# One DMA for the gate and up weights, and the softmax normalisation recorded ahead of the transposes

## What is computed

```python
# DIM 1024, 16 heads of 64, window 256, HIDDEN 3072
q = x @ q_w.T; kv = x @ kv_w.T; k, v = kv[..., :64], kv[..., 64:]
attn = softmax(einsum('bhnwd,bnud->bhnwu', qb, kb) * 64**-0.5)
out  = einsum('bhnwu,bnud->bhnwd', attn, vb)            # per window
x = layernorm(x + out @ proj_w.T + proj_b)
h = silu(x @ w_gate.T / 127) * (x @ w_up.T / 127)       # int8 weights
x = layernorm(x + h @ w_down.T / 127)
```

## Time and profile before

| | |
|---|---|
| two timed runs | 998.68 and 1094.42 us, median 1046.55 us |
| profiled execution, time | 997.76 us |
| its span on the slowest core (core 3 of eight; 987.5 to 995.9 us) | 995.9 us |
| PE busy | 829.3 us (83%) |
| DVE busy | 322.5 us (32%) |
| ACT busy | 241.7 us (24%) |
| POOL busy | 118.1 us (12%) |
| mean granted TensorE clock of a core | 0.89 to 0.90 |

### The profile page before, as it was taken

How to read it: one execution, slowest core, us unless ns; L and a number is a source line. 1 busy time by engine, 2 the same in 40 slices (tenths; PEclk the granted TensorE clock), 3 DMA queues, 4 the chain that set the end, 5 groups by cost and what they waited for, 6 DMA issues and landing times.

```text
span 995.9 us, 12616 instructions; the slowest of 8 cores (987.5 to 995.9 us)
## 1 busy us (share of the span) xinstructions
PE 829.3 (83%) x4288; PEld 362.3 (36%) x4288; DVE 322.5 (32%) x538; ACT 241.7 (24%) x745; POOL 118.1 (12%) x232
## 2 busy tenths in 40 slices
PE   6767776767989999956888899767798999999996
PEld 6123333222434444412333334323243444443332
DVE  0146767332222212102445546533222221111111
ACT  0054545112121111102333334411212111111111
POOL 2000010000222223200000010000122222310000
PEclk9567777797999999977999999778899999999999
DMA  8950120114434445372211130112443444530121
GB/s 117 271 125 12 22 54 1 64 64 137 134 121 129 137 148 157 119 116 51 51 43 43 43 85 33 43 57 79 129 147 107 141 145 150 157 107 32 64 81 68
DMA packets 46957, 94.15 MB, mean 95 GB/s; under 512 B 5552, under 2 KB 5552, under 8 KB 46896
## 3 DMA queue, kind: packets, MB, share of 16 engines
q0 software_dynamic: 37520, 67.91, 26.7%
q1 hardware_dynamic: 9376, 25.43, 7.8%
HBM read 63.44 MB, written 12.58 MB: 76 GB/s over the span
## 4 chain that ended last, share of the span: by engine, by line
PE 64%; DVE 11%; DMA 11%; issue 8%; ACT 5%; DVEq 0%; SPq 0%; POOL 0%; ACTq 0%; POOLq 0%
PE ps L264 60%; DMA wqsb<-wq 5%; PE ps L381 4%; DMA x<-xtm 4%; DVE pool L366 3%; DMA xbf<-xfm 2%; DVE silu L710 2%; ACT r L718 2%; DVE r L710 1%; ACT silu L718 1%; DVE pool L389 1%; DVE x2s L728 1%; DVE pool L320 1%; DVE xbf L456 1%; DVE hbuf L594 1%
## 5 line engine op out<-in xcount | busy, mean ns | idle before, releaser
L264 PE MATMUL ps<-xbf,wuw 128*128 128x512 bf16 x768 | 186.6, 387 | 14.1 <-DVE hbuf L594 14.1
L264 PE MATMUL ps<-xbf,wgw 128*128 128x512 bf16 x768 | 184.3, 383 | 10.6 <-DVE xbf L456 10.6
L264 PE MATMUL ps<-wdres,hbuf 128*128 128x512 bf16 x768 | 186.7, 389 | 7.6 <-PE ps L264 0.3
L594 DVE SCALAR_TENSOR_TENSOR hbuf<-ps,silu 128x512 bf16<-128x512 f32 x96 | 66.4, 692 | 271.7 <-PE ps L264 267.4
L349 ACT ACTIVATE pool<-ps 128x256 bf16<-128x256 f32 x256 | 98.2, 384 | 134.9 <-PE ps L264 89.5
L589 ACT ACTIVATE silu<-ps 128x512 f32<-128x512 f32 x96 | 56.9, 597 | 279.3 <-PE ps L264 279.3
L264 PEld LDWEIGHTS ps<-xbf,wuw 128*128 128x128 bf16 x768 | 75.6, 99 | 108.5 <-issue 21.1
L264 PEld LDWEIGHTS ps<-xbf,wgw 128*128 128x128 bf16 x768 | 75.4, 99 | 104.9 <-issue 19.2
L264 PEld LDWEIGHTS ps<-wdres,hbuf 128*128 128x128 bf16 x768 | 70.6, 99 | 113.3 <-issue 43.8
L564 POOL DMA_DIRECT2D wgw<-wg x96 | 50.8, 529 | 352.4 <-PE ps L264 352.4
L264 PE MATMUL ps<-xbf,wqsb 128*128 128x512 bf16 x256 | 77.4, 445 | 4.1 <-DVE pool L320 0.9
(11 more groups left out here) (55 smaller groups left out, 350.3 us busy)
## 6 DMA issues: line engine op xcount, KB each, us to landing
wgw<-wg POOLq DMA_DIRECT2D x96, 256.0 KB, 2.6
wuw<-wu POOLq DMA_DIRECT2D x96, 256.0 KB, 2.6
x<-xtm SPq DMA_DIRECT2D x16, 512.0 KB, 3.7
y<-x SPq DMA_DIRECT2D x16, 512.0 KB, 2.9
wdres<-wd POOLq DMA_DIRECT2D x1, 6144.0 KB, 50.1
wqsb<-wq POOLq DMA_DIRECT2D x18, 256.0 KB, 4.0
xbf<-xfm POOLq DMA_DIRECT2D x2, 2048.0 KB, 18.4
x2scr<-x2s SPq DMA_DIRECT2D x16, 256.0 KB, 2.2
```

Source lines behind the costliest of these rows:

```text
L264: last = t.matmul(o, l, r, start=st_, stop=sp, tile_position=tpos)
L594: return v.scalar_tensor_tensor(H_sb[:, m, n * 512:(n + 1) * 512], bank(6)[:, 0:512], FS, silu_sb[:, par, n * 512:(n + 1) * 512], ALU.mult ...
```

## The change

There are two edits, which do not touch each other.

**Weights.** The two DRAM tensors `wg` and `wu` become one, `wgu`, with gate and up side by side for each `m` (put together on the host); the two SBUF tensors become one, `wguw`; and the two loads of a unit become one DMA. Its slot is `wgu0` or `wgu1`. G and U of a unit both wait for that one DMA, and the DMA waits for both G and U of unit `m-2`.

**Attention.** In a stage, `emit_norm` now comes ahead of `emit_AT`. The norm has DVE work only, so PE's, ACT's and SP's operations keep their order.

```diff
-    wg_d = nc.dram_tensor("wg", [HC, 128, DC * 128], I8, kind="ExternalInput").ap()
-    wu_d = nc.dram_tensor("wu", [HC, 128, DC * 128], I8, kind="ExternalInput").ap()
+    wgu_d = nc.dram_tensor("wgu", [HC, 2, 128, DC * 128], I8,
+                           kind="ExternalInput").ap()
...
-        wgw_sb = sb("wgw", [128, 2, DC, 128], BF16)
-        wuw_sb = sb("wuw", [128, 2, DC, 128], BF16)
+        wguw_sb = sb("wguw", [128, 2, 2, DC, 128], BF16)
...
+                    if 1 <= i <= NCH:
+                        j, b = divmod(i - 1, NBLK)
+                        emit_norm(j, b)
                     if 2 <= i <= NCH + 1:
                         j, b = divmod(i - 2, NBLK)
                         emit_AT(j, b)
-                    if 1 <= i <= NCH:
-                        j, b = divmod(i - 1, NBLK)
-                        emit_norm(j, b)
...
-        def emit_ffn_w(st, m, which, dst_sb, src_d):
-            def fn(g, m=m, dst_sb=dst_sb, src_d=src_d):
+        def emit_ffn_w(st, m):
+            def fn(g, m=m):
                 return g.dma_start(
-                    dst_sb[:, m % 2, :, :],
-                    src_d[m, :, :].rearrange("p (k f) -> p k f", k=DC))
-            P.dma("gd", f"{which}{m % 2}", fn, reads=(),
-                  writes=(f"{which}{m % 2}",), note=f"ld {which} m{m} st{st}")
+                    wguw_sb[:, m % 2, :, :, :],
+                    wgu_d[m, :, :, :].rearrange("q p (k f) -> p q k f", k=DC))
+            P.dma("gd", f"wgu{m % 2}", fn, reads=(),
+                  writes=(f"wgu{m % 2}",), note=f"ld wgu m{m} st{st}")
...
-            mm_group(g_pairs, f"G m{m} n{n}", reads=XC + (f"wg{par}",),
+            mm_group(g_pairs, f"G m{m} n{n}", reads=XC + (f"wgu{par}",),
...
-            mm_group(u_pairs, f"U m{m} n{n}", reads=XC + (f"wu{par}",),
+            mm_group(u_pairs, f"U m{m} n{n}", reads=XC + (f"wgu{par}",),
...
-                emit_ffn_w(st, m + 2, "wg", wgw_sb, wg_d)
-                emit_ffn_w(st, m + 2, "wu", wuw_sb, wu_d)
+                emit_ffn_w(st, m + 2)
```

More of the change, by code:

```diff
@@ L528, in emit_projseg @@
             for m in range(2):
-                emit_ffn_w(st, m, "wg", wgw_sb, wg_d)
-                emit_ffn_w(st, m, "wu", wuw_sb, wu_d)
+                emit_ffn_w(st, m)
             for wt in range(2, 4):
@@ L554, in emit_projseg @@
             emit_x2t(st, NBLK * 2 - 1)
[L555 to L558, removed]
+            emit_ffn_w(st, 0)
+            emit_ffn_w(st, 1)
             for m in range(HC):
                 gu_unit(st, m, 1)
-        def emit_ffn_w(st, m, which, dst_sb, src_d):
-            def fn(g, m=m, dst_sb=dst_sb, src_d=src_d):
+        def emit_ffn_w(st, m):
+            def fn(g, m=m):
                 return g.dma_start(
-                    dst_sb[:, m % 2, :, :],
-                    src_d[m, :, :].rearrange("p (k f) -> p k f", k=DC))
-            P.dma("gd", f"{which}{m % 2}", fn, reads=(),
-                  writes=(f"{which}{m % 2}",), note=f"ld {which} m{m} st{st}")
+                    wguw_sb[:, m % 2, :, :, :],
+                    wgu_d[m, :, :, :].rearrange("q p (k f) -> p q k f", k=DC))
+            P.dma("gd", f"wgu{m % 2}", fn, reads=(),
+                  writes=(f"wgu{m % 2}",), note=f"ld wgu m{m} st{st}")
         def gu_unit(st, m, n):
@@ L574, in gu_unit @@
             for k in range(DC):
-                g_pairs.append((bank(gb)[:, 0:512], wgw_sb[:, par, k, :],
+                g_pairs.append((bank(gb)[:, 0:512], wguw_sb[:, par, 0, k, :],
                                 xbf_sb[:, k, n * 512:(n + 1) * 512],
                                 k == 0, k == DC - 1, None))
-                u_pairs.append((bank(6)[:, 0:512], wuw_sb[:, par, k, :],
+                u_pairs.append((bank(6)[:, 0:512], wguw_sb[:, par, 1, k, :],
                                 xbf_sb[:, k, n * 512:(n + 1) * 512],
                                 k == 0, k == DC - 1, None))
-            mm_group(g_pairs, f"G m{m} n{n}", reads=XC + (f"wg{par}",),
+            mm_group(g_pairs, f"G m{m} n{n}", reads=XC + (f"wgu{par}",),
                      writes=(f"pb{gb}",))
-            mm_group(u_pairs, f"U m{m} n{n}", reads=XC + (f"wu{par}",),
+            mm_group(u_pairs, f"U m{m} n{n}", reads=XC + (f"wgu{par}",),
                      writes=("pb6",))
             if m + 2 < HC:
-                emit_ffn_w(st, m + 2, "wg", wgw_sb, wg_d)
-                emit_ffn_w(st, m + 2, "wu", wuw_sb, wu_d)
+                emit_ffn_w(st, m + 2)
             def silu_fn(s_, par=par, n=n, gb=gb):
@@ L752 @@
     wuT = tile_w(np.asarray(L0_ffn_w_up, dtype=np.int32).astype(np.int8).T, 24, 8)
+    wguT = np.ascontiguousarray(np.stack([wgT, wuT], axis=1))
     wdT = np.ascontiguousarray(
@@ L765 @@
             "xtm": xs, "xfm": xfs, "wq": wqT, "wkv": wkvT, "wp": wpT,
-            "brep": brep, "wg": wgT, "wu": wuT, "wd": wdT,
+            "brep": brep, "wgu": wguT, "wd": wdT,
         })
```

## The result

The changed kernel is **slower**: 1030.38 us (median) against 1001.55 us, ratio 1.0294, 95% interval 1.0277 to 1.0312. That is 29 us more where 8 were forecast (1006 against 997.8), and just above the range's upper end of 1029.

What follows compares the result with a forecast made beforehand. PE was taken to bound the gate/up passes, and a chain of waits (normalisation, PE's transposes, DVE's copy) the attention. The terms summed as 997.8 - 22 + 30 = 1006 us, range 984 to 1029.

Steps and rivals of the forecast that it cites:

- Edit 1: Attention: normalisation ahead of the transposes' copy takes DVE's wait for transposes away; gains 22 us (bounds 14 and 44).
- The part beside the down projection: Attention running beside the down projection, and its rest: earlier normalisation frees `E` earlier; forecast change -5 us.
- Edit 2: Gate/up passes: one DMA for both weights makes PE stop 38 times for 0.8 us; costs 30 us (bounds 11 and 41).
- L: Merged 512 KB weight load's time from issue to landing; forecast 3.4 us, with bounds 2.9 and 3.7.
- the release: Gate/up: the 0.14 us from a load's landing to PE's start, taking the 2.75 us left to 2.61.
- The count of stops: Gate/up passes: one stop for two units, 11 in each n = 1 pass and 8 in each n = 0, 38 in all.
- My rule: Gate/up passes: PE is late by L - 2.61 at one unit, and the next unit's load is just in time.
- B: Merged weight load lands later because POOL writes both halves before the first moves; 1017 us at L = 3.7; chance 0.15.
- A: Merged weight load is in time, or denser attention keeps full clock; 976 us, down to 965; chance 0.14.
- C: Attention edit does nothing for the time, since exponentials and not the copy hold the pipeline; 1028 us; chance 0.07.
- The sum: Whole kernel: 997.8 - 22 + 30 = 1006 us, from the profiled execution's own time.

Runs made afterwards that it cites:

- third buffer: Changed kernel with three weight buffers in turn, so the merged load is issued one unit earlier: 979.16 us, ratio 0.9796 to the kernel before.
- two late loads: Changed kernel's attention with two 256 KB weight loads, the gate load also waiting for the up matmuls: 991.41 us, ratio 0.9906 to the kernel before.
- opposite order: Kernel before with each attention stage ordered transposes, value product, normalisation: 1011.11 us, ratio 1.0116 to the kernel before.

## Why the prediction was wrong

- **What bounds the kernel: right.** Passes with nothing to spare on PE, attention bound by the chain from normalisation to transposes to copy.
- **Edit 1, 22 us: right, the sum in part by luck.** By stretches it was 21, alone on the chip 20 (1001.02 to 981.42). I had replayed one period of 16.46 us, one of the long kind, to 14.73 at mixed clocks and about 11.8 at full clock, and charged 7 periods of 2.0, 14 us. There are 6, and their mean fell by 2.3, 14 us as well. The clock rose with the denser work, from 0.75 to 0.86, which is between the two cases that I had replayed, and about half of the gain came with it. The part beside the down projection was 3 and not 5.
- **Edit 2, the mechanism: right.** About one stop for two units, PE late by L - 2.61, the release 0.14. The third buffer and the two late loads show each half of it.
- **Edit 2, the size: wrong, and here the prediction failed.** The step was "L = 2.6 + 0.65 and about 0.15 for twice the rows to write: 3.4". L was 3.7. The 0.65 came from loads that were queued behind one another, and 256 KB more in a load that starts on an idle queue cost 0.85: the packets took 1.87 us instead of 1.01. By the packet records the middle half of the merged load's bytes passed in 0.63 us, at the rate of the queued loads, and its first and last quarters took 0.60 and 0.52; that queued loads hide such slow ends behind each other is how I read it, not shown. The rows cost 0.17 to 0.2, near the 0.15 that I had put, but no row of the kernel before had shown that term. With 3.7 the same formula gives 1.09 us for a stop and 41 us in all. The row of the 512 KB loads on the other queue read the same 3.7, and I had kept it for the upper bound; that may be chance, since it reads 3.9 in the changed kernel.
- **The count of stops, and one landing time for all loads: wrong, and smaller.** I counted 38; there were 42 to 51. A load slower than the median also stops an odd unit, which in my count was just in time, and from there on the stops fall on the odd units until a slow load shifts them back. By the matmuls' starts about as many odd units were late as even ones (25 to 34 and 25 to 31 on a core, on the six cores whose matmul records are complete). By the landing records, one in ten of the loads within a pass took over 3.9 to 4.5 us, by core, and the longest 5.9. My rule, replayed for an n = 1 pass, gives 12.0 us lost with 3.7 for every load and 13.9 in the mean with each load's own landing time; measured were 14.7. So the spread is most of the step from 41 to 47 us, and some 0.8 us a pass stay open. The experiment with two late loads prices this by itself: loads with the median at the limit, no regular stop, and 10 us lost. I had put one landing time on all loads.
- **Rivals.** B was the nearest, with L = 3.7, but its 1017 us had the same count, and its reason, the writing of both halves ahead of the first packet, was 0.2 of the 1.1 us. It put the end of "no measurable change" at L above 3.7, and with the slow loads counted it lies at about 3.5 (1021.78 us with L = 3.5). A and C were both wrong.
- **The sum.** 8 us more was a small difference of two large terms, -22 and +30, so an error of 17 in one made the forecast change less than a third of the measured one.
- The *Trainium skill*, page *DMA: Bandwidth & Descriptors*, section on the anatomy of one DMA, has a fit that gives, as an estimate, 3.2 us for 512 KB. The trace agreed at 256 KB (2.6) and not here (3.7, or 3.5 with the rows in one piece); the measurement decides.

## What to carry to other kernels

When two transfers are merged, the first half starts when the second could have, and the whole lands when the last byte does; so before counting what a merge saves, compare issue-to-landing of the merged size, on an idle queue, with the time that its buffer leaves. Where that is close, price the slow loads too and not the median alone, or give the buffer one more stage. In a software pipeline whose engines take their work in order, put the operation whose input is ready ahead of the one that waits for another engine: here three moved lines gave 1.75% (ratio 0.9825).

## What was not expected of the hardware

- Two halves in one DMA of 256 rows landed 0.2 us later than the same bytes in 128 rows of twice the length (3.7 and 3.5); POOL's instruction was 0.70 against 0.53 us. In a loop without slack this alone was worth 8.6 us.
- 256 KB more on an idle queue cost 0.85 us (packets 1.87 against 1.01), behind a load already under way 0.65 (landings of queued loads).
- TensorE's clock followed the waits in the attention: 0.70 with the opposite order (row below, columns as in the earlier trace rows), 0.75 before, 0.86 with the new one, with the same instructions on PE.

```profile
64.00:175.00 111.00, 77.50 (x522) 34.84 (x519) 70.41 (x120) 50.02 (x212) 4.76 (x9) 0.70 0.12 22
```
